# Graph attention and mixture of experts on one core: node-stage transfers of 125 rows cut into 112 and 13

## What is computed

```python
def gnn(node_features, edge_index, Wp, a_src, a_trg, Wskip, bias):
    N, E, FIN, H, FO = (6250, 100000, 256, 8, 32)
    x = node_features
    src, trg = (edge_index[0], edge_index[1])
    proj = (x @ Wp.T).reshape(-1, H, FO)
    scores_src = jnp.sum(proj * a_src, axis=-1)
    scores_trg = jnp.sum(proj * a_trg, axis=-1)
    s = jax.nn.leaky_relu(scores_src[src] + scores_trg[trg], negative_slope=0.2)
    exp_s = jnp.exp(s - jnp.max(s))
    denom = jax.ops.segment_sum(exp_s, trg, num_segments=N)
    attn = exp_s / (denom[trg] + 1e-16)
    out = jax.ops.segment_sum(proj[src] * attn[:, :, None], trg, num_segments=N)
    out = out + (x @ Wskip.T).reshape(-1, H, FO)
    return jax.nn.elu(out.reshape(-1, H * FO) + bias)

x = x + gnn(layernorm(x), stack([src, dst]), ...)   # 6250 nodes of 256, 200000 edges
x = x + ffn(layernorm(x), ...)                      # top 2 of 8 experts, 256 -> 1024 -> 256
```

## Time and profile before

| | |
|---|---|
| runs, median (lowest to highest) | 3188.27 us (3187.75 to 3189.39) |
| the profiled execution | 3191.06 us, its span from first to last instruction 3189.4 us |
| mean granted TensorE clock | 0.817 |
| node stage | from about 62 us to 244 us of the span |
| edge stage | from 244 us to about 2230 us |

### The profile page before, as it was taken

One profiled execution on the slowest core, in us unless ns is written; L12 is line 12 of the kernel. 1 busy time (PEld: TensorE's weight loads), 2 busy tenths in 40 slices (PEclk: granted clock), 3 DMA queues, 4 the chain that ended last, 5 costly groups with the idle time before them and its releaser, 6 DMA issues. The chain is left out here.

```text
span 3189.4 us, 46614 instructions
## 1 busy us (share of the span) xinstructions
PE 2071.1 (65%) x12432; PEld 1745.7 (55%) x12433; DVE 1937.4 (61%) x5386; ACT 861.3 (27%) x2271; POOL 1775.1 (56%) x1829
## 2 busy tenths in 40 slices
PE   3775666666666666666666666665342999999990
PEld 2444444444444444444444444444332999999980
DVE  6545666666666666666666666666783665656655
ACT  1222222222221112222222221111441555555540
POOL 1006777777777777777777777775475222212110
PEclk7997887878888888888878787777555999999995
DMA  1333444444444444444444444443444222212117
GB/s 44 112 110 101 109 108 108 109 108 108 109 108 108 109 108 108 109 108 108 109 108 108 109 108 108 109 108 83 136 138 137 66 79 64 86 56 73 41 43 241
DMA packets 192452, 327.35 MB, mean 103 GB/s; under 512 B 70287, under 2 KB 124542, under 8 KB 192428
## 3 DMA queue, kind: packets, MB, share of 16 engines
q0 software_dynamic: 98560, 256.53, 29.4%
q1 hardware_dynamic: 74328, 51.16, 5.7%
q10 hardware_dynamic: 19540, 19.40, 1.9%
HBM read 278.03 MB, written 47.99 MB: 102 GB/s over the span
## 5 line engine op out<-in xcount | busy, mean ns | idle before, releaser
L620 POOL DMA_INDIRECT rows<-proj_table,idx x1568 | 1486.3, 948 | 711.1 <-issue 418.2
L665 PE MATMUL banks<-weighed,onehot 128*128 128x264 f32 x3136 | 1082.8, 504 | 740.3 <-DVE weighed L736 739.5
L665 PEld LDWEIGHTS banks<-weighed,onehot 128*128 128x128 f32 x3136 | 735.5, 246 | 913.9 <-issue 767.6
L840 ACT ACTIVATE banks<-score,neg_bound 128x32 f32<-128x32 f32 x392 | 114.1, 291 | 1572.5 <-DVE score L729 1572.5
L726 DVE TENSOR_TENSOR raw_score<-rows,target 128x32 f32<-128x32 f32 x392 | 75.3, 192 | 717.4 <-DMA rows<-proj_table,idx 715.2
L736 DVE TENSOR_TENSOR weighed<-rows,banks 128x1024 f32<-128x1024 f32 x392 | 473.6, 1208 | 0.0
L1456 POOL DMA_INDIRECT results_by_token<-yrow,goes_to x104 | 108.9, 1047 | 478.6 <-DVE yrow L1404 350.4
L1343 ACT ACTIVATE hid<-banks,params 128x256 f32<-128x256 f32 x416 | 198.1, 478 | 267.7 <-PE banks L1299 261.1
L702 DVE TENSOR_TENSOR onehot<-banks,key_tab 128x512 f32<-128x512 f32 x397 | 270.1, 681 | 0.0
L1392 DVE TENSOR_TENSOR hidl<-hid,hidh 128x256 fp32r<-128x256 f32 x416 | 169.8, 424 | 149.7 <-ACT hidh L1337 149.5
L1299 PE MATMUL banks<-f_xth,w1h 128*128 128x256 f32 x832 | 236.4, 284 | 28.0 <-ACT hid L1343 14.5
(11 more groups left out here) (235 smaller groups left out, 2871.5 us busy)
## 6 DMA issues: line engine op xcount, KB each, us to landing
rows<-proj_table,idx POOLq DMA_INDIRECT x1568
w_raw<-in_L_ffn_W_dram POOLq DMA_DIRECT2D x16, 1024.0 KB, 6.3
xrow<-tokens_by_expert SPq DMA_DIRECT2D x106, 128.5 KB, 2.1
c_y<-results_by_token SPq DMA_DIRECT2D x10, 1120.0 KB
proj_table<-trow ACTq DMA_DIRECT2D x50, 128.9 KB
xin<-in_x_dram SPq DMA_DIRECT2D x50, 125.0 KB
skip_rows<-srow ACTq DMA_DIRECT2D x50, 125.0 KB
r_skin<-skip_rows SPq DMA_DIRECT2D x10, 625.0 KB
```

Of the source, the lines that this page charges most:

```text
L620: nc.gpsimd.indirect_dma_start(rows[k][:, i, :], None, table, bass.IndirectOffsetOnAxis(ap=idx[pair][:, col:col + 1], axis=0)).then_inc(ga ...
L665: mm = nc.tensor.matmul(acc_bank[u // 2 % 2][:, 0:ROW], onehot[u][:, i, :], weighed[:, k * SET + i, :], start=(u % 2 == 0 and i == 0), sto ...
```

## The change

Each transfer of the node stage that moved 125 partitions is now two, one of partitions 0 to 111 and one of 112 to 124. SP issues the loads, ACT all the stores, as before. Both parts count on the semaphore that the whole counted on, so the waits are for 32 where they were for 16. Nothing else is changed: the same bytes go to the same places.

```diff
+def part_of(t, part):
+    return bass.ds(t * NP + part.start, part.stop - part.start)
...
-                    sp.dma_start(xin[:, u, :], x[tile(2 * i + u), :]).then_inc(x_loaded[u], 16)
+                    for part in NODE_PARTS:
+                        sp.dma_start(xin[part, u, :], x[part_of(2 * i + u, part), :]).then_inc(x_loaded[u], 16)
...
-                    dve.wait_ge(x_loaded[u], 16 * (i + 1))
+                    dve.wait_ge(x_loaded[u], 16 * len(NODE_PARTS) * (i + 1))
...
-                    dve.wait_ge(srow_stored[u], 16 * i)
-                    dve.wait_ge(trow_stored[u], 16 * i)
+                    dve.wait_ge(srow_stored[u], 16 * len(NODE_PARTS) * i)
+                    dve.wait_ge(trow_stored[u], 16 * len(NODE_PARTS) * i)
...
-                act.wait_ge(trow_stored[u], 16 * i)
+                act.wait_ge(trow_stored[u], 16 * len(NODE_PARTS) * i)
...
-                act.dma_start(table[tile(t), :], trow[:, u, :]).then_inc(trow_stored[u], 16)
-                act.dma_start(skip_rows[tile(t), :], srow[:, u, :]).then_inc(srow_stored[u], 16)
+                for part in NODE_PARTS:
+                    act.dma_start(table[part_of(t, part), :], trow[part, u, :]).then_inc(trow_stored[u], 16)
+                for part in NODE_PARTS:
+                    act.dma_start(skip_rows[part_of(t, part), :], srow[part, u, :]).then_inc(srow_stored[u], 16)
```

More of the change, by code:

```diff
@@ L542, in _ @@
             for u in range(2):
-                act.wait_ge(trow_stored[u], 16 * (NT // 2))
-                act.wait_ge(srow_stored[u], 16 * (NT // 2))
+                act.wait_ge(trow_stored[u], 16 * len(NODE_PARTS) * (NT // 2))
+                act.wait_ge(srow_stored[u], 16 * len(NODE_PARTS) * (NT // 2))
 def edge_phase(nc, m, bank, table):
```

## The result

The changed kernel takes 3203.7 us (median of 5, 3201.56 to 3204.27), the kernel before 3188.27 (5 runs). The ratio is 1.0045, 95% interval 1.0034 to 1.0056: 11 to 18 us more. Forecast were 3211 us and slower; the sign and the mechanism held, the size was 22.9 us where about 14 were measured (by the ratio; the medians lie 15.4 apart).

What follows compares the result with a forecast made beforehand. Transfers on about five DMA engines were taken to set the node stage's 6.92 us round. First stores +2.2, 22 rounds +18.0, clock +4.4, last pass -0.5 and end -1.2 gave +22.9: 3211 us, range 3194 to 3232.

Steps and rivals of the forecast that it cites:

- The pace before: Node stage: transfers on about five engines set the 6.92 us round, read from waits for stores and DMA share 0.34.
- the term for the loads: Node stage, SP: four load issues for two cost nothing, since a load is wanted about a round later.
- The step that decided: Node stage: waits for stores go to zero; eight issues in series on ACT, ahead of the next `std`, set the round.
- The round: Node stage loop: 7.74 us for 6.92, with eight issues at 0.333 us; +18.0 us over 22 rounds.
- The clock: TensorE in the node stage: longer idle spells bring more lower clock, 0.2 us a round, +4.4 us in all.
- The start: First stores to second round of the node stage: four new issues and four dearer ones, +2.2 us.
- The end: Last `std` to next stage: wait gone in the last pass, -0.5 us, and -1.2 us after it.
- Issues at 0.268 for all parts: Rival, ACT's issues in the node stage: spreading costs nothing, round 7.22 us, 3194 us; chance 0.10.
- issuing nearly free: Rival, node stage: round falls towards 5.54 us, total 3155 us, faster; chance 0.05.
- no change: Rival, node stage: a cheaper issue step leaves the round about 6.9 to 7.0 us, within 6 us of 3188; chance 0.04.
- TensorE at the lower clock: Rival, node stage: TensorE stays at the lower clock, round 9.1 us, total 3238 us; chance 0.05.
- unspread parts: Rival, node stage: cut parts stay on about five engines, round 8.0 us, total 3217 us; chance 0.04.

Runs made afterwards that it cites:

- e5: Kernel before with nothing cut, its stores to skip_rows issued by SP instead of ACT: 3189.91 us, ratio 1.0004 to the kernel before.
- e10: Kernel before, no transfer cut, with four buffers for trow and srow in place of two: 3195.36 us, ratio 1.0003 to the kernel before.
- e1: Changed kernel with only the loads cut, all stores whole again: 3172.97 us, ratio 0.9945 to the kernel before.
- e2: Changed kernel with only the stores cut, the loads whole again: 3204.2 us, ratio 1.0043 to the kernel before.
- e3: Changed kernel with the stores to skip_rows whole again, six issues a round on ACT: 3177.56 us, ratio 0.9958 to the kernel before.
- e4: Changed kernel, all transfers still cut, with the stores to skip_rows issued by SP instead of ACT: 3155.74 us, ratio 0.989 to the kernel before.
- e6: Changed kernel with its cut at 100 instead of 112, so parts of 100 and 25: 3193.2 us, ratio 1.0013 to the kernel before.
- e8: e1 (only loads cut) with four buffers for trow and srow in place of two: 3168.16 us, ratio 0.9921 to the kernel before.
- e9: Changed kernel with table stores whole on ACT, skip_rows stores cut but issued by SP, four trow and srow buffers: 3151.31 us, ratio 0.987 to the kernel before.

## Why the prediction was right, and where its terms were off

*The pace before.* Right, but one of its two legs was weak. That the transfers set the 6.92 us is shown by e5 (fewer issues, same round) and e10 (more time to land, same round). The DMA share of 0.34 alone did not show it: in the changed kernel it is 0.36, though no engine waits for a transfer. I had forecast that it would fall below 0.34; that sign was wrong. That about five engines carried everything is borne out by the packet records of the traces, 80 to 180 us: before, five or six packets are in flight for 90% of the time and fewer than four for 0.2%; now there are up to 21, and none for 38% of the time. A packet of a row took 46 ns (median), and 150 rows a round on each of five engines are 6.9 us.

One wait of the kernel before was overlooked (80 to 230 us):

```profile
DVE stats L392 <- DMA xin<-in_x_dram: 9.3, 22, 0.5
```

Once a round DVE stood for a load as well: it was not the stores alone that landed late. In the loop this cost the forecast nothing, since with the loads cut the wait is gone, as the term for the loads has it, and ACT's issues set the pace. What cutting the loads is worth by itself, 0.67 us a round, e1 shows.

*The step that decided.* Right: waits for stores to zero, eight issues in series on ACT, `std` behind them. e2, e3, e4 and e6 show it from four sides: the stores alone lose it all, two issues less give 1.08 us, the same transfers from two queues give 1.94 us, and cheaper issues give their sum.

*The round, 7.74 forecast, 7.55 measured, 7.51 in most rounds.* The price of an issue was taken from a 128-row load at 0.333; it is 0.323 for both parts. The term most mis-sized is the lead from `trow` to the first issue: 0.23 forecast, 0.05 now (147.78 to 147.83). I took it from a `trow` that waited for a transfer; there the queue did the address work of that issue only afterwards (at 148.95, `trow` having started at 148.78). At the first stores of the trace before it stood at 73.43, ahead of `trow` at 73.45, and the first issue came at once, in a row that I had left out:

```profile
73.49 0.60 ACTq L526 DMA_DIRECT2D proj_table<-trow  x1
```

That is 4 of the 8.4 us by which the 22 rounds fell short. The clock, below, is 3.5, and the cheaper issues, 0.08 us a round, are 1.8; smaller terms go both ways, such as the step between issues, 0.16 and not 0.155.

*The clock, +4.4 forecast, about +0.9 measured.* TensorE was granted the lower level more often, as expected (0.90 and 0.91 for 1.00 and 0.93). But three in four rounds kept 7.51 or 7.52, and the mean of 22 is 0.04 above that. Twelve rounds had the full clock and took 7.51 to 7.53; of the ten that were partly at the lower level (0.77 or 0.78 over the round) five kept 7.51 or 7.52, and five took 7.55 to 7.77. I had written that a round half at the lower clock stays inside TensorE's idle time, and then charged a share of the worst case all the same. What the lower level costs hangs on where it falls: in the round shown under the result it fell on the second transpose, 0.64 us for 0.43, for which ACT waits.

*The start, +2.2 forecast, +0.4 measured.* The eight issues of the first stores cost what was forecast (the first pass of the loop is 9.81 us from `std` to `std`, 7.56 before: +2.25). What was missing is the gain of the cut loads, which I had put at nothing: nothing in the loop, but at the start the first `std` comes 0.95 us earlier, and from it to the loop's first `std` it is 4.14 us for 5.03. Both go with the loads. The second is 3.89 to 4.14 us in all eight kernels here with cut loads, 4.75 to 5.05 in the four with whole ones. The first `std` waits for seven loads of weights that SP issues ahead of its loop: from the issue of the last of them to DVE's first work on them it is 4.23 us before and 3.14 now, 4.1 to 4.5 with whole loads behind them and 2.7 to 3.5 with cut ones.

*The end* was right (-1.5 for -1.7, of it -0.5 as forecast in the last pass). *Later stages* gave -1.7 us in the profiled pair, nearly all in the edge stage (1983.3 for 1985.3 us); over all the kernels here, which do not touch it, that stage took 1982 to 1989 us, so I count this as scatter.

*Rivals.* Issues at 0.268 for all parts and issuing nearly free are refuted by the rows, no change by the interval, TensorE at the lower clock by the 0.90 granted, and unspread parts by the waits and the count of packets (e6). The Trainium skill (DMA: Bandwidth & Descriptors, Issuing engines are not separate DMA queues) says that initiating transfers on several engines saves only the time of initiating, and that this is usually small beside the transfer. The first half is what e4 measured: four issues with their address work, 4 x 0.483 = 1.93 us, left ACT, and the round fell by 1.94. The second half speaks of one transfer, here 0.48 us beside the 2.1 that a 128-row load takes to land; but it is the sum that counts here: eight issues in series with computing are 3.8 of 7.55 us on ACT.

## What to carry to other kernels

Before a transfer is cut to spread it, find out which list issues it and what stands behind it there: an issue is work of that engine (here 0.27 to 0.32 us, and 0.16 until the next), in series with its computing. Cut what an idle queue issues (the loads on SP: 0.55% faster), leave whole or move what a busy one issues (both: 1.3% faster). And take the price of a moved step from a row in which the engine did not wait for what the change removes.

## What the runs showed that I had not expected

- In these five cases the price of an issue went by how its rows divide and not by how many they are: 0.268 us for 125 and for 25 rows, 0.292 for 100, 0.323 for 112 and for 13.
- The same bytes kept the DMA engines busy longer when spread: a share of 0.34 over a round of 6.92 us before, 0.36 over 7.55 after, so about 16% more busy time a round (0.36 x 7.55 against 0.34 x 6.92). A packet of a row took 55.5 ns on average, for 48.9. It cost nothing here.
- The edge stage, whose code is the same in all of them, took 1988.5 and 1989.1 us in e8 and e9 and 1982.3 to 1985.3 in the other profiles. What makes it so is open. The group of e8 to e10 ran on another chip, on which the kernel before takes 2 to 5 us more as well; e10's profile, with 1983.7 us there, is that of its fastest execution, 5.8 us under its median.
